# Layer-1 attention scores as 64-row products in two row tiles of TensorE, in place of stacked 128-row products

## The reference, cut to what matters

```python
hn = _group_norm(x, gamma, beta)
q = _conv1x1(hn, wq, bq).reshape(b, NH, HD, hw)        # NH = 4, HD = 64, hw = 1024
k = _conv1x1(hn, wk, bk).reshape(b, NH, HD, hw)
v = _conv1x1(hn, wv, bv).reshape(b, NH, HD, hw)
attn = jnp.einsum('bhdq,bhdk->bhqk', q, k) * scale
attn = jax.nn.softmax(attn, axis=-1)
out = jnp.einsum('bhqk,bhdk->bhdq', attn, v)
return x + _conv1x1(out.reshape(b, c, h, w), wp, bp)
```

## Time and profile before

| | |
|---|---|
| median of 3 runs | 724.21 us (723.22 to 724.33) |
| span of the profiled execution | 718.7 us |
| TensorE busy | 696.6 us, 97% of the span |
| TensorE loading weights | 591.1 us, 82% |
| VectorE, ScalarE, GpSimd busy | 537.1, 454.8, 229.3 us |
| mean granted TensorE clock | 0.998 |

### The profile page before, as it was taken

One profiled execution on the slowest core, in us unless ns is written; L12 is line 12 of the kernel. 1 busy time (PEld: TensorE's weight loads), 2 busy tenths in 40 slices (PEclk: granted clock), 3 DMA queues, 4 the chain that ended last, 5 costly groups with the idle time before them and its releaser, 6 DMA issues.

```text
span 718.7 us, 11880 instructions
## 1 busy us (share of the span) xinstructions
PE 696.6 (97%) x3888; PEld 591.1 (82%) x3888; DVE 537.1 (75%) x878; ACT 454.8 (63%) x820; POOL 229.3 (32%) x214
## 2 busy tenths in 40 slices
PE   5999999999999988999999999999999999999996
PEld 4888888888888877887888887887987888888885
DVE  4665366455557636999888889888889988889994
ACT  4552254154235415798777788877779878768883
POOL 0120121022013202366332446423346533334430
PEclk9999999999999999999999999999999999999999
DMA  8001300130130164600256300165401155401010
GB/s 277 1 2 43 110 24 15 44 117 0 44 131 1 46 171 106 178 1 1 73 133 161 104 31 31 45 161 132 132 15 44 44 119 125 122 16 45 13 44 33
DMA packets 29100, 52.72 MB, mean 73 GB/s; under 512 B 3456, under 2 KB 5760, under 8 KB 29056
## 3 DMA queue, kind: packets, MB, share of 16 engines
q1 hardware_dynamic: 29056, 52.19, 26.3%
HBM read 18.62 MB, written 8.39 MB: 38 GB/s over the span
## 4 chain that ended last, share of the span: by engine, by line
PE 88%; DVE 4%; ACT 3%; issue 2%; DMA 2%; SPq 0%; ACTq 0%; DVEq 0%
PE acc L1093 44%; PE scores L1093 26%; PE trans L1127 18%; DVE negmax L775 2%; DVE pt_lo L793 1%; DMA w_later<-in_wlater 1%; ACT prob L582 1%; ACT pt_hi L592 1%; DVE o_sum L996 0%; DMA q_st<-qk 0%; ACT o_sum L696 0%; ACT h_hi L640 0%; DVE gn_sqdev L829 0%; DVE rsum L780 0%; SPq L382 0%
## 5 line engine op out<-in xcount | busy, mean ns | idle before, releaser
L502 POOL TENSOR_SCALAR prob<-prob,rsum 128x1024 f32<-128x1024 f32 x159 | 179.2, 1127 | 472.2 <-DVE rsum L780 472.2
L592 ACT ACTIVATE pt_hi<-trans 128x512 fp32r<-128x512 f32 x320 | 174.8, 595 | 134.2 <-PE trans L1127 131.7
L775 DVE TENSOR_REDUCE negmax<-scores 128x1 f32<-128x1024 f32 x160 | 194.3, 1214 | 49.1 <-PE scores L1093 47.4
L793 DVE TENSOR_TENSOR pt_lo<-trans,pt_hi 128x512 fp32r<-128x512 f32 x320 | 204.6, 681 | 10.8 <-ACT pt_hi L592 10.5
L582 ACT ACTIVATE prob<-scores,negmax 128x1024 f32<-128x1024 f32 x160 | 179.1, 1119 | 30.1 <-DVE negmax L775 28.5
L1127 PEld LDWEIGHTS trans<-ident,prob 128*128 128x128 f32 x1280 | 147.0, 140 | 31.7 <-DVE pt_lo L793 5.1
L1127 PE MATMUL trans<-ident,prob 128*128 128x128 f32 x1280 | 168.7, 274 | 3.5 <-DVE pt_lo L793 3.1
L1093 PE MATMUL scores<-k_st,q_st 128*128 128x512 f32 x512 | 138.4, 392 | 3.9 <-DMA q_st<-qk 3.9
L1093 PEld LDWEIGHTS scores<-k_st,q_st 128*128 128x128 f32 x512 | 96.4, 189 | 25.1 <-DMA q_st<-qk 4.3
L1093 PE MATMUL acc<-pt_hi,v_st 128*128 128x512 f32 (+1 forms) x264 | 106.6, 406 | 1.8 <-DVE pt_lo L793 1.8
L1093 PE MATMUL acc<-pt_lo,v_st 128*128 128x512 f32 (+1 forms) x264 | 101.0, 385 | 0.0
(11 more groups left out here) (119 smaller groups left out, 864.6 us busy)
## 6 DMA issues: line engine op xcount, KB each, us to landing
k_st<-qk SPq DMA_DIRECT2D x64, 256.0 KB, 4.6
q_st<-qk SPq DMA_DIRECT2D x64, 128.0 KB, 2.4
x_raw<-in_x SPq DMA_DIRECT2D x8, 512.0 KB, 6.7
y_out<-in_x SPq DMA_DIRECT2D x16, 256.0 KB, 3.8
y_scratch<-y_out SPq DMA_DIRECT2D x16, 256.0 KB, 2.0
y_in<-y_scratch SPq DMA_DIRECT2D x4, 1024.0 KB, 7.4
y_res<-y_scratch SPq DMA_DIRECT2D x16, 256.0 KB, 3.6
out<-y_res SPq DMA_DIRECT2D x16, 256.0 KB, 2.0
```

What stands on the lines that cost most here:

```text
L502: nc.gpsimd.tensor_scalar(p, p, rsum[:, t % 2:t % 2 + 1], 1.0, ALU.mult, ALU.mult)\
L592: nc.scalar.activation(pt_block(pt_hi, (t // 4) % 2, t, h), trans[:, h, :].rearrange("p (j n) -> p j n", n=P), ACT.Copy).then_inc(pt_high, 1)
L775: nc.vector.tensor_reduce(negmax[:, t % 2:t % 2 + 1], scores[:, t % 2, :], AX_X, ALU.max, negate=True).then_inc(max_ready, 1)
L793: nc.vector.tensor_tensor(pt_block(pt_lo, slot, t, h), trans[:, h, :].rearrange("p (j n) -> p j n", n=P), pt_block(pt_hi, slot, t, h).bitc ...
```

## The change

`q_st` and `k_st` keep their total size, but `q_st` now has both parts of q in both halves of the partitions, and `k_st` has, in the partitions 0 to 63, the keys of the first half, and in 64 to 127 those of the second half, both parts each. A step's scores are three products (high by high, low by high, high by low) of 64 rows for each half of the keys: those of the first half use the array's rows 0 to 63, those of the second half its rows 64 to 127, in turn. Low by low, which the stacked form made as well, is no longer made. A q chunk is moved by four DMAs of both parts, a k chunk by two.

```diff
-        q_st = sb("q_st", [P, HEADS, N], F32R)
-        k_st = sb("k_st", [P, 2, HEADS, N], F32R)
+        q_st = sb("q_st", [P, 2, HEADS, N], F32R)
+        k_st = sb("k_st", [P, 2, HEADS, H], F32R)
...
-        CHUNK_DMA = 4 * 16
-        QK_IMAGE = 4 * CHUNK_DMA
+        Q_DMA, K_DMA = 4 * 16, 2 * 16
+        QK_PAIR = Q_DMA + K_DMA
+        QK_IMAGE = PAIRS * QK_PAIR
+
+        def stacked_before(r):
+
+            return (r // 4) * QK_PAIR + (Q_DMA if r % 4 >= 2 else 0)
...
                 for n in range(2):
-                    head, rows = 2 * pair + n, slice(n * HD, (n + 1) * HD)
-                    for u in range(2):
-                        if is_k:
-                            dst, src = k_st[u * HD:(u + 1) * HD, :, head, cols], qk[rows, slot, :, :]
-                        else:
-                            dst, src = q_st[u * HD:(u + 1) * HD, head, cols], qk[rows, slot, u, :]
+                    head, src = 2 * pair + n, qk[n * HD:(n + 1) * HD, slot, :, :]
+                    if is_k:
+                        homes = [k_st[half * HD:(half + 1) * HD, :, head, :]]
+                    else:
+                        homes = [q_st[u * HD:(u + 1) * HD, :, head, cols] for u in range(2)]
+                    for dst in homes:
                         sp.dma_start(dst.bitcast(F32), src.bitcast(F32)).then_inc(qk_stacked[slot], 16)
...
-                act.wait_ge(qk_stacked[r % 2], FREE_CREDIT + QK_IMAGE * i + CHUNK_DMA * (r // 2))
+                act.wait_ge(qk_stacked[r % 2], FREE_CREDIT + QK_IMAGE * i + stacked_before(r))
...
-                        pe.wait_ge(qk_stacked[slot], FREE_CREDIT + QK_IMAGE * i + CHUNK_DMA * (2 if s == 0 else 4))
+                        pe.wait_ge(qk_stacked[slot], FREE_CREDIT + QK_IMAGE * i + QK_PAIR * (1 if s == 0 else 2))
                 pe.wait_ge(exp_ready, t1 + s + 1)
-                for mh in range(2):
-                    ins = run(scores[:, s % 2, col(mh, H)],
-                              [(q_st[:, head, col(tile, P)], k_st[:, part, head, col(mh, H)]) for part in range(2)])
+                terms = products((q_st[:, 0], k_st[:, 0]), (q_st[:, 1], k_st[:, 1]))
+                for n, (q, k) in enumerate(terms):
+                    for mh in range(2):
+                        rows = slice(mh * HD, (mh + 1) * HD)
+                        ins = nc.tensor.matmul(scores[:, s % 2, col(mh, H)], q[rows, head, col(tile, P)], k[rows, head, :],
+                                               start=n == 0, stop=n == len(terms) - 1)
                 ins.then_inc(scores_ready, 1)
```

## The result

The changed kernel takes 734.27 us (median of 4 runs, 731.94 to 735.89), the kernel before 723.74 us in the same comparison: a ratio of 1.0138, with a 95% interval of 1.0123 to 1.0152. It is slower by 1.4%, 10 us. The profiled execution has a span of 733.6 us and took 735.4 us, so 1.8 us lie around the program. If as much lies around the program before, its profiled execution took about 720.5 us and was some 3 us faster than its median, so the 5.5 us which I put around the span were not all of that kind. Some 2 of the 3 us are the program's start: TensorE's last product of layer 0 begins at 266.80 us in the profile of before and at 268.75 in that of the changed kernel, though TensorE's work up to there is the same; the lead is there within the first 20 us.

What follows compares the result with a forecast made beforehand. TensorE, busy 97% of the span, was taken to bound the kernel. The four terms summed as -18.8 + 3.2 - 4.8 + 2.4 = -18.0 us, from 724.2 to 706.2 us, with a range of 695 to 745 us.

Steps and rivals of the forecast that it cites:

- the 5.5 us which I put around the span: Whole kernel: the runs' median stands 5.5 us above the profiled span, so a 700.7 us span means 706.2.
- What bounds the kernel: Whole kernel: TensorE, busy 97% of the span, sets the time; VectorE is next in line, with 12% to spare.
- Term 1, that the tiles run side by side: Layer 1 scores: six 64-row products take three slots of 0.227 us, 0.68 a step in place of 0.91.
- Term 1, what the borders cost: Layer 1 steps: full-array to half-array work and back costs 0.08 us a step, leaving -18.8 us over 128 steps.
- Term 2, VectorE's chain: Layer 1 steps without projection: the 2.64 us maximum-exponential-reciprocal chain hides part of the saving, giving back 3.2 us.
- Term 3, the entry: Entry into layer 1: TensorE's wait shrinks from 3.9 to about 0.8 us, the low clock behind goes: -4.8 us.
- Term 4, ScalarE's wait for the q chunk: Images 1 to 3: ScalarE waits about 1 us for larger q DMAs before rewriting their slot: +2.4 us.
- the second, the border that drains: Layer 1 scores: TensorE empties at both borders, 0.33 us a step; +11.2 us in sum, 735 us; chance 0.20.
- The first (loads bind): Layer 1 scores: 64-row weight loads cost 0.140 us, a step saves 0.07; 713 us; chance 0.57 together with the forecast.
- the third (no overlap): Layer 1 scores: TensorE takes the six products one by one, +58 us; 780 us; chance 0.11.

Runs made afterwards that it cites:

- the fourth pair: The changed kernel with the low by low product added as one more pair of 64-row products a step: 761.84 us.
- one pair: Layout of the kernel before, with two full-array score products and then two 64-row products a step in place of four full-array ones: 736.13 us, ratio 1.0173.
- three in a row: The changed kernel with the three products of the first tile issued before the three of the second: 734.84 us, ratio 1.0143.
- the DMAs alone: The changed kernel's layout and DMAs, but with four 128-row score products a step as before: 726.21 us, ratio 1.0037.
- the small q chunk: The changed kernel's two-DMA k chunks with four 128-row products, each q chunk cut to half the bytes, as before the change: 719.06 us, ratio 0.9929.
- the control: The kernel before, with the fourth 128-row score product of each step moved between the two halves of the transposes: 737.34 us, ratio 1.0175.
- the kernel better than both: The kernel before, with restacking DMAs counted apart by head so first scores wait for the first head's only: 718.97 us, again 719.41 us.
- the products alone: The kernel before, its data layout and DMAs kept, with the six 64-row score products a step: 734.74 us, ratio 1.0142.
- the split pairs: The changed kernel with the last two of each step's six 64-row products moved between the two halves of the transposes: 777.37 us.

## Why the prediction was wrong

The forecast was 706.2 us; 734.3 was measured, within the range but on the other side of 724. By its steps:

- **What bounds the kernel**: right. TensorE is still busy for 97%, and what a step got longer by came through: 0.12 us in a plain step, 3.6 us in the 32 steps of image 1 (114.00 against 110.38).
- **Term 1, that the tiles run side by side**: right. Three slots in place of four, shown by the six products in 0.96 us and by the fourth pair at 0.22 us.
- **Term 1, what the borders cost**: this is the step that failed. I took 0.08 us a step from the row of the first `av` product behind the transposes, "the only one that shows a border between two kinds of work in steady flow". It is 0.33 to 0.36, four times that: 0.1 in, 0.11 for bare weights behind it, 0.10 out, 0.05 for the next load. That row was no border of the kind in question: both sides use the whole array. Nor does it show a cost: the eight transposes and the step to the first `av` product take 437.29 - 436.49 = 0.80 us, 0.07 less than eight slots of 0.109, and the 0.08 that the next product comes late only gives this back. The error was to prefer the nearest row to a bound when that row showed something else. In the sum, 128 x (0.35 - 0.08) = 35 us more than forecast turn the term from -19 us into about +16.
- **Term 2, VectorE's chain**: it did not come to bear, since steps became longer. VectorE was to be 92% busy; it is busy for 98.70 of image 1's 114.00, 87%.
- **Term 3, the entry**: right, and a little small. The wait went to nothing (0.8 was forecast) and the clock behind it stays up. Alone, with the q chunk small, it is worth 5 us (4.8 forecast). The steps to the 0.8 us don't add up: 253.83 + 6.7 is 260.5 and not 261.5, and 1 us behind 262.64 is 263.6 and not 263.1. ScalarE's write came 0.5 us late, not 1.
- **Term 4, ScalarE's wait for the q chunk**: right in mechanism and place, wrong in size. The wait was put at 1 us, three times, and 2.4 us in all; with steps as short as before it is 2.65, 0.99 and 0.96 us, and the q chunk's size costs 7 us, part of it through the longer stop. In the changed kernel, with longer steps, the wait is about 0.45 us each time, but the stop of ScalarE in image 2 and, in this execution, the low clock behind it come on top, some 4 us. I had not seen that stop, although the trace of before has it with 2 us.
- **The rivals**: what came was the second, the border that drains, given 0.20 with 735 us; its price per step, 0.33, is what was measured, to 0.03. That its figures fit so well is partly luck: it had 0.165 us for each border and no bare load, where about 0.1 and, for the loads, 0.16 a step were measured, and its 735 us leave out the stop in image 2. The first (loads bind) is excluded by the fourth pair, the third (no overlap) by the trace.

The chances were the weak point: the row held against the draining border (0.08) measured no such border, so no row spoke against that rival, yet I gave it 1 in 5.

## What to carry to other kernels

Row tiles on 64 rows do give two products in one slot, but each visit to them from full-array work costs as much as one and a half slots, here about 0.35 us, with one pair in it as with three. By that price, as an estimate, a visit must save two slots (0.45 us) to pay, which no run here tried; with one saved, as here, it loses. Nor was a kernel tried in which the work beside the scores is of 64 rows too, so that there is no border. And where a change makes a transfer larger, look at who waits to write its source again, and at what runs beside the transfer, not only at who waits for its data.

## What the runs showed of the hardware that was not expected

- The weight loads of the two tiles run beside each other as the products do: in the changed kernel six of them, 0.184 us each, cover 0.53 us of a step, and the two of a pair start 3 to 4 ns apart. Two 64-row loads cost no more than one.
- Products of the second tile start beside those of the first even when three of the first tile are issued ahead of them (0.97 us for six, either way), if the pairs are read as above. The Trainium skill (TensorE: Matmul & The Clock Gate, Part 3) says that products start and end strictly in program order; by that reading, this run does not agree with it across row tiles.
- After TensorE had stood still for about 3 us in image 2, the clock fell for 6.8 us (the changed kernel, 2.93 us; the fourth pair, 3.01), for 3.4 us (three in a row, 2.90) or not at all (the DMAs alone, 3.11). So waits of about one length were followed by a long low stretch, a short one or none.
- ScalarE stops once, early in image 2, in the same place in every profile. With q chunks of 0.5 MB it stands for 2.0 to 2.15 us (before, the small q chunk, one pair, the control, the kernel better than both; in the products alone 2.05 us, put down to transposes of which it needed the first four, and those had ended 1.4 us earlier). With q chunks of 1 MB it is 3.9 to 5.0 us (4.0 in the changed kernel and the DMAs alone, 3.9 with three in a row, 4.9 in the split pairs, 5.0 with the fourth pair). It is where ScalarE's loop over images goes round for the first time. In all twelve traces an 8 KB packet of the DMA queue of kind "instruction" (q14) starts within the stop, 1.7 to 1.9 us before its end with the small chunks and 2.2 to 2.3 with the large ones. So fetching instructions through the same DMA engines could be the cause; no run here tests it, and it stays open.
